# Flamingo block on one Trainium2 core: the first rounds' scores and weight splits and the last rounds' banks and VectorE list put in another order

## The chip, the cores and the metric

The kernel runs on one core of one Trainium2 chip. The metric is the device time of one execution in microseconds. The median of three timed runs counts; a profiled execution has its own time and a trace.

## The reference

For each of 32 batch entries (called tiles here: 128 tokens by 256 features) the reference computes two blocks, one behind the other:

```
x = x + tanh(g_xattn) * xattn(layernorm(x), ctx, ctx, mask)        # 16 heads of 16, called A
x = x + tanh(g_ffn)   * ffn(layernorm(x))                          # called B, below
ffn(y): q, k from rope(y), v from y; causal softmax attention, 16 heads; out projection
        x1 = layernorm(y + attention)
        gates = softmax(x1 @ gate_w.T + gate_b); the 2 largest of 8 are kept
        moe = sum over experts of gate_e * (x1 @ expert_w[e].T + expert_b[e])
        return layernorm(x1 + moe)
```

The softmax subtracts each row's maximum, and float32 accuracy is kept by splitting every operand of a large product into a high and a low part (three products in place of one).

## The kernel before

One tile is one batch entry. The work of a tile is cut into steps (a small function each), and each engine has one handwritten list of steps inside `for r in rounds`. A round advances two tiles; the 32 tiles take 21 rounds (r = 0 to 20), because a step of tile t stands in the round that its lag gives it (`scores("A", 2 * r - 1)`). A step for a tile below 0 or above 31 does nothing. So in the first and last rounds most of the list is empty, and `if r == ...` lines put things there that exist only at that end. Every engine works strictly in its list's order; semaphores say what a step waits for.

Names of the steps, with the tile in brackets behind them in this text: A0 is cross attention of tile 0, B31 causal attention of tile 31.

- Scores need the four **score banks** of PSUM (banks 0 to 3), one tile's attention at a time, in the fixed order A, B, A, B (`SCORES`). For each: ScalarE *seeds* the banks with the mask (`seed_scores`), TensorE adds the scores (`scores`, L516), VectorE takes the maxima (`maxima`, L1022), for A ScalarE seeds again with the transposed mask (`seed_scores_t`, L785), TensorE makes the transposed scores (`scores_t`, L535), the maxima are cast into two bfloat16 parts (`max_parts`, L1034 and L1036), transposed (`transpose_max`, L546, and `max_transposed`, L818), subtracted (`subtract_max`, L556), and ScalarE takes the exponentials (`exponentials`, L826). Only then can the next seed overwrite the banks.
- The four **work banks** (4 to 7) hold everything else: projections, products with the values (`attend`, L574, kept by `raw_values`, L834), `normalise` (L585), the expert products (`expert_pair`, L395). `WORK_USES` fixes their order; `take_work` waits until the last reader of the bank is done.
- **Splits**: each of the 16 weight matrices (Ak, Av, Aq, Ao, Bk, Bq, Bv, Bo, E0 to E7) arrives in one of six staging buffers; ScalarE makes the high part (`split_high`, L750), VectorE the low part (`split_low`, L933). They happen in the first rounds only. SyncE's queue loads a weight when the buffer's last low part is made.
- **keep_busy** (L411): products of the identity with itself, into a free work bank, whose result nobody reads. They stand where TensorE would be idle.
- After B's output projection (`project_o`, `finish_b`), the steps of a tile are: `statistics("1")`, GpSimd's `inverse_root`, `apply_u` (L964), GpSimd's `scale_shift_u`, `u_transposed` and its parts, `gate` (L595 on TensorE, L1077 on VectorE), `gate_rank`, `gate_choice`, `transpose_gates`, `gates_low` (L1115), `expert_bias_sum`, `bias_sum` (L1122), four `expert_pair` and eight `expert_sum` (L1131), `statistics("2")`, `apply_v` (L964, v_n) and `finish` on GpSimd, then the store. `rope` stands on GpSimd between `apply_y` (yn) and `rope_transposed`.

Of the kernel before, what the change touches and what calls it, by code (L numbers as in the profile page):

```python
# [30 lines left out]
PAIR = 2  # L31
# [104 lines left out]
def build(nc, dram, out):  # L136
    tiles = out.shape[0]
    with ExitStack() as ctx:
# [98 lines left out]

        def work_bank(use, n):

            key = (use, None) if (use, None) in WORK_AT else (use, n % PAIR)  # L240
            return work_banks[WORK_USES[WORK_AT[key]][2]]

        def work_last(use, n):
# [4 lines left out]
            while turn >= 0:  # L248
                _, half, other_bank, behind, readers = WORK_USES[turn % len(WORK_USES)]
                pair = turn // len(WORK_USES) - behind  # L250
                if other_bank == bank and live(PAIR * pair):
# [133 lines left out]
        def tensor_program(pe):  # L385
            def take_work(use, t):
                for name, value in work_last(use, t):
                    pe.wait_ge(sem[name], value)
                return work_bank(use, t)
# [40 lines left out]
            def u_transposed(t):  # L430
# [3 lines left out]
                transpose_two(take_work("u_t", t), u[t % U_SLOTS], "u_t", t)  # L434
# [192 lines left out]
            for r in rounds:  # L627
                gate(2 * r - 6)
                project_v_b(2 * r - 4)
                if r == 1:  # L630
                    keep_busy("x_t", 2, 3)
# [4 lines left out]
                project_o("B", 2 * r - 5)  # L636
                attend("B", 2 * r - 4)
                scores("A", 2 * r - 1)
                if r == 18:
                    keep_busy("gates_t", 30, 4)  # L640
                transpose_gates(2 * r - 6)
                expert_pair(0, 2 * r - 6)
                expert_bias_sum(2 * r - 6)
                expert_pair(1, 2 * r - 6)
                expert_pair(2, 2 * r - 6)
                if r == 1:
                    keep_busy("A_v", 2, 15)
                if r == 2:
                    keep_busy("A_v", 4, 13)
                scores_t("A", 2 * r - 1)  # L650
                transpose_max("A", 2 * r - 1)
                rope_transposed(2 * r - 2)
                subtract_max("A", 2 * r - 1)
                normalise("B", 2 * r - 4)
                expert_pair(3, 2 * r - 6)
                o_transposed("B", 2 * r - 4)
                if r == 1:
                    keep_busy("A_v", 2, 4)
                attend("A", 2 * r - 1)
                u_transposed(2 * r - 5)  # L660
                y_transposed(2 * r - 3)
                if r == 2:
                    keep_busy("A_v", 4, 4)
# [3 lines left out]
                project_k_a(r)  # L667
                if r == 18:
                    keep_busy("pair0", 31, 8)
                gate(2 * r - 5)  # L670
                normalise("A", 2 * r - 1)
                project_v_a(2 * r)
# [3 lines left out]
                transpose_max("B", 2 * r - 3)  # L676
                o_transposed("A", 2 * r - 1)
                if r == 0:
                    keep_busy("A_max_t", 0, 6)
                x_t(2 * r + 1)  # L680
# [7 lines left out]
                project_q_a(r)  # L688
# [5 lines left out]
                if r == 1:  # L694
                    keep_busy("rope_t", 1, 3)
# [6 lines left out]
                expert_bias_sum(2 * r - 5)  # L702
# [770 lines left out]
```

## Time and profile before

| what | value |
|---|---|
| median of 3 runs | 829.06 us (829.02 to 829.14) |
| the profiled execution's own time | 831.21 us |
| its span, first to last instruction | 829.5 us |
| PE (TensorE matmul) busy | 779.7 us, 94% of the span |
| DVE (VectorE) busy | 667.5 us, 80% |
| ACT (ScalarE) busy | 564.4 us, 68% |
| POOL (GpSimd) busy | 473.0 us, 57% |
| mean granted TensorE clock | 0.994 of full speed |

Times in the trace are microseconds from the start of the span. The busy share of PE includes the keep_busy products, so a busy PE is not yet a PE that sets the time. A row of the timeline gives start, duration, engine, line and operation; what stands in brackets is the idle time ahead of it on its engine and who ended it.

### The profile page before, as it was taken

How to read it: one execution, taken by the hardware profiler on the slowest of the kernel's cores; microseconds unless marked ns; L12 is line 12 of the kernel's file. 1: busy time of each engine (PE TensorE's matmuls, PEld its weight loads, DVE VectorE, ACT ScalarE, POOL GpSimd, SP SyncE). 2: the span in 40 equal slices, each digit the busy share in tenths (PEclk: the TensorE clock that was granted, in tenths of full speed). 3: DMA queues.
4: the chain of work that ended last, by engine and by line, in shares of the span. 5: the costliest groups of instructions: out<-in, count | busy, mean ns of one | idle time of the engine just before them, and what ended most of it. 6: DMA issues, size and time to landing. Idle time of an engine off the chain costs nothing.

```text
span 829.5 us, 24325 instructions
## 1 busy us (share of the span) xinstructions
PE 779.7 (94%) x9515; PEld 611.9 (74%) x9515; DVE 667.5 (80%) x1908; ACT 564.4 (68%) x1268; POOL 473.0 (57%) x854
## 2 busy tenths in 40 slices
PE   8888989999999999999999999999999999999896
PEld 4465768777787787778787788778778777777663
DVE  5756668797978979797988979797988979787876
ACT  5786767777786777777776777678677777764320
POOL 8434535566665646566574646566564655555343
PEclk9999999999999999999999999999999999999999
DMA  7510000010100101010100101010010000000000
GB/s 202 159 39 16 2 17 16 8 37 9 37 8 2 37 8 36 9 36 9 29 16 2 38 8 37 8 37 9 10 35 2 9 8 8 9 8 8 8 7 20
DMA packets 33570, 20.75 MB, mean 25 GB/s; under 512 B 11672, under 2 KB 33456, under 8 KB 33456
## 3 DMA queue, kind: packets, MB, share of 16 engines
q1 hardware_dynamic: 33456, 19.19, 8.1%
q8 instruction: 76, 1.25, 0.6%
q14 instruction: 38, 0.31, 0.1%
HBM read 14.99 MB, written 4.19 MB: 23 GB/s over the span
## 4 chain that ended last, share of the span: by engine, by line
PE 56%; ACT 24%; DVE 14%; issue 4%; POOL 1%; DMA 0%; SPq 0%; DVEq 0%; POOLq 0%
PE bank L395 26%; PE bank L516 8%; PE bank L535 7%; ACT bank L776 6%; DVE neg_max_A L1022 6%; ACT bank L785 5%; DVE moe L1131 4%; ACT probs_B L826 3%; PE bank L556 3%; PE bank L585 3%; ACT probs_A L826 3%; PE bank L574 2%; PE bank L404 2%; ACT k_heads_B L809 2%; PE bank L546 1%
## 5 line engine op out<-in xcount | busy, mean ns | idle before, releaser
L1343 POOL TENSOR_SCALAR_AFFINE_SELECT probs_B<-probs_B 128x512 f32<-128x512 f32 x128 | 77.3, 640 | 184.4 <-ACT probs_B L826 184.4
L1131 DVE SCALAR_TENSOR_TENSOR moe<-bank,gates,moe 128x256 f32<-128x256 f32 x256 | 123.2, 481 | 48.2 <-PE bank L395 33.2
L785 ACT ACTIVATE bank<-mask_add 128x512 f32<-128x512 bf16 x128 | 76.6, 602 | 49.2 <-DVE neg_max_A L1022 49.2
L395 PE MATMUL bank<-w_expertsa,u_t_a 128*128 128x512 f32 x256 | 105.6, 413 | 0.1
L395 PE MATMUL bank<-w_expertsa,u_t_b 128*128 128x512 f32 x256 | 100.9, 394 | 0.0
L395 PE MATMUL bank<-w_expertsb,u_t_a 128*128 128x512 f32 x256 | 100.9, 394 | 0.0
L1022 DVE TENSOR_REDUCE neg_max_A<-bank 128x4 f32<-128x512 f32 x128 | 79.5, 684 | 11.9 <-PE bank L516 11.5
L1022 DVE TENSOR_REDUCE neg_max_B<-bank 128x4 f32<-128x512 f32 x128 | 79.3, 682 | 5.5 <-PE bank L516 5.5
L776 ACT ACTIVATE bank<-mask_add 128x512 f32<-128x512 bf16 x128 | 69.8, 626 | 0.0
L776 ACT ACTIVATE bank<-causal_add 128x512 f32<-128x512 bf16 x128 | 69.7, 623 | 0.0
L826 ACT ACTIVATE probs_A<-bank 128x512 f32<-128x512 f32 x128 | 66.1, 603 | 4.4 <-PE bank L556 2.2
L826 ACT ACTIVATE probs_B<-bank 128x512 f32<-128x512 f32 x128 | 66.2, 607 | 3.2 <-PE bank L556 1.1
L834 ACT ACTIVATE o_raw<-bank 128x512 f32<-128x512 f32 x64 | 38.5, 602 | 27.8 <-PE bank L574 27.8
L395 PEld LDWEIGHTS bank<-w_expertsa,u_t_a 128*128 128x128 f32 x256 | 49.1, 192 | 10.6 <-issue 0.4
L1260 POOL TENSOR_SCALAR var_eps<-mean_var 128x1 f32<-128x1 f32 x64 | 12.3, 192 | 77.7 <-DVE mean_var L960 75.2
L395 PEld LDWEIGHTS bank<-w_expertsa,u_t_b 128*128 128x128 f32 x256 | 48.1, 188 | 11.4
L395 PEld LDWEIGHTS bank<-w_expertsb,u_t_a 128*128 128x128 f32 x256 | 48.3, 189 | 6.7
L535 PEld LDWEIGHTS bank<-q_heads_A,k_heads_A 32*128 32x128 f32 x1024 | 31.4, 186 | 22.4 <-ACT bank L785 22.4
L809 ACT ACTIVATE k_heads_A<-bank,k_cols_A,head_rows 128x256 f32<-128x256 f32 x64 | 30.9, 565 | 23.0 <-PE bank L395 23.0
L535 PE MATMUL bank<-q_heads_A,k_heads_A 32*128 32x128 f32 x1024 | 37.5, 283 | 8.1 <-ACT bank L785 7.4
L411 PE MATMUL bank<-ident_bf 128*128 128x512 bf16 x167 | 42.7, 396 | 1.9 <-ACT k_heads_B L809 1.9
L516 PE MATMUL bank<-k_heads_A,q_heads_A 32*128 32x256 f32 x512 | 36.7, 399 | 5.8 <-ACT bank L776 4.7
(224 smaller groups left out, 2440.5 us busy)
## 6 DMA issues: line engine op xcount, KB each, us to landing
x_in<-in_x SPq DMA_DIRECT2D x32, 128.0 KB, 2.2
ctx_t<-in_ctxT SPq DMA_DIRECT2D x32, 128.0 KB, 2.2
out<-y_out SPq DMA_DIRECT2D x32, 128.0 KB, 1.7
w_stage<-in_expertsT SPq DMA_DIRECT2D x8, 256.0 KB, 4.3
mask_u<-in_masks SPq DMA_DIRECT2D x32, 32.0 KB, 2.1
w_stage<-in_in_projT SPq DMA_DIRECT2D x3, 256.0 KB, 4.8
w_stage<-in_WkT SPq DMA_DIRECT2D x1, 256.0 KB, 3.5
w_stage<-in_WvT SPq DMA_DIRECT2D x1, 256.0 KB, 3.6
```

The costliest lines, as they stand in the source:

```text
L395: done = pe.matmul(out_ap, l, r, start=n == 0, stop=n == len(terms) - 1)
L411: pe.matmul(bank[:], ident_bf[:], ident_bf[:].unsqueeze(1).to_broadcast([P, GROUP, P]), start=True, stop=True)
L516: done = pe.matmul(score_banks[g][:, c * 2 * P:(c + 1) * 2 * P], queries[strip, half, c, :], keys[strip, half, c, :, :], start=False, stop ...
L535: pe.matmul(score_banks[g][:, i * P:(i + 1) * P], keys[strip, half, c, odd, :], queries[strip, half, c, :], start=tag == "B" and i == 0, s ...
L776: act.activation(score_banks[g][:].rearrange("p (h k) -> p h k", k=P), mask[:, 0:1, :].to_broadcast([P, GROUP, P]), ACT.Copy).then_inc(sem ...
L785: act.activation(score_banks[g][:].rearrange("p (h k) -> p h k", k=P), mask_add[t % MASK_SLOTS][:, 1:2, :].to_broadcast([P, GROUP, P]), AC ...
L809: act.activation(k_heads[tag][pair % PAIR_SLOTS][:, :, c, odd, :], bank[:, c * PAIR * P:(c + 1) * PAIR * P].rearrange("p (j n) -> p j n", ...
L826: act.activation(probs[tag][:, g * GROUP:(g + 1) * GROUP, :].rearrange("p h q -> p (h q)"), score_banks[g][:], ACT.Exp, scale=SCALE).then_ ...
L834: act.activation(o_raw[:], work_bank(tag + "_values", t)[:], ACT.Copy).then_inc(sem[tag + "_or"], 1)
L1022: dve.tensor_reduce(neg_max[tag][:, g * GROUP:(g + 1) * GROUP], score_banks[g][:].rearrange("p (h k) -> p h k", k=P), AXIS_X, ALU.max, neg ...
L1131: dve.scalar_tensor_tensor(out=moe[(e + 1) % 2][:], in0=bank[:, (e % 2) * EMBED:(e % 2 + 1) * EMBED], scalar=gates[:, e:e + 1], in1=moe[e ...
L1343: pool.affine_select(out=part, in_=part, compare_op=ALU.is_ge, fill=0.0, base=0, pattern=[[0, GROUP], [1, P]], channel_multiplier=-1).then ...
```

## The change

It rewrites the lists at both ends; the rounds between stay as they are but for one wait on `u_transposed` that goes.

First rounds (r = 0 to 4). On TensorE the scores of A1 stand ahead of A0's output projection, transpose_max of A0 and A1 ahead of their scores_t, project_k_a(1) ahead of attend of A1, x_t(3) ahead of normalise of A1, rope_transposed(0) far behind, project_q_a(1) ahead of project_o of A1. keep_busy counts change (8 in place of 3 between that project_o and the scores of A2; 4 moved from ahead of B1's scores to ahead of A3's). On ScalarE and VectorE the splits and the gate's small parts move to other places.

Last rounds (r = 17 to 20). Six uses of work banks by the last tiles (`LATE`) go to score banks, which nobody seeds again. With that, tile 31's normalise, transpose, output projection and u_transposed move ahead on TensorE, and VectorE's list takes the steps of tiles 29 to 31 in a new order; GpSimd's `scale_shift_u` stands ahead of `finish` in r = 19.

```diff
+        LATE = {("B_normalise", tiles - 1): (0, "B_exp", GROUPS * tiles), ("B_o_t", tiles - 1): (1, "B_exp", GROUPS * tiles),
+                ("B_out", tiles - 1): (2, "B_exp", GROUPS * tiles), ("pair3", tiles - 3): (3, "B_exp", GROUPS * tiles),
+                ("u_t", tiles - 1): (0, "B_on", tiles), ("gate", tiles - 1): (1, "B_ot_b", tiles)}
+
         def work_bank(use, n):
 
+            if (use, n) in LATE:
+                return score_banks[LATE[use, n][0]]
...
             def take_work(use, t):
+                if (use, t) in LATE:
+                    pe.wait_ge(sem[LATE[use, t][1]], LATE[use, t][2])
+                    return work_bank(use, t)
...
                 pe.wait_ge(sem["u"], t + 1)
-                transpose_two(take_work("u_t", t), u[t % U_SLOTS], "u_t", t)
+                transpose_two(work_bank("u_t", t), u[t % U_SLOTS], "u_t", t)
...
                 if r == 1:
-                    keep_busy("x_t", 2, 3)
+                    keep_busy("x_t", 2, 2)
+                if r == 1:
+                    scores("A", 2 * r - 1)
                 project_o("A", 2 * r - 2)
...
                 attend("B", 2 * r - 4)
-                scores("A", 2 * r - 1)
...
+                if r == 2:
+                    keep_busy("A_v", 4, 4)
+                if r != 1:
+                    scores("A", 2 * r - 1)
...
                 y_transposed(2 * r - 3)
-                if r == 2:
-                    keep_busy("A_v", 4, 4)
                 scores("B", 2 * r - 3)
...
                 if r == 1:
-                    keep_busy("rope_t", 1, 5)
+                    keep_busy("A_values", 2, 3)
+                if r == 1:
+                    project_q_a(r)
                 project_o("A", 2 * r - 1)
...
                 if r == 1:
-                    keep_busy("rope_t", 1, 3)
+                    keep_busy("A_values", 2, 8)
...
                 if r == 18:
                     keep_busy("pair1", 31, 3)
                 expert_bias_sum(2 * r - 5)
+                if r == 17:
+                    normalise("B", 2 * r - 3)
                 expert_pair(1, 2 * r - 5)
...
+                if r == 17:
+                    o_transposed("B", 2 * r - 3)
...
                 expert_pair(3, 2 * r - 5)
+                if r == 17:
+                    u_transposed(2 * r - 4)
+                if r == 17:
+                    project_o("B", 2 * r - 3)
...
+                if use == "u_t" and t >= tiles - 2:
+                    act.wait_ge(sem[read[0]], read[1] * t)
...
+                if t == tiles - 2:
+                    dve.wait_ge(sem["vn"], t)
                 dve.tensor_tensor(moe[0][:], work_bank("bias", t)[:, 0:EMBED], u[t % U_SLOTS][:], ALU.add).then_inc(
                     sem["moe"], 1)
```

**ScalarE (ACT), tiles 0 and 1.** The rows from the transposed maxima of A0 to the exponentials of A1 (neg_max_t, probs, o_raw; L776 is the seed, L785 the second seed, L750 a high split; xn_t_a belongs to tile 2, rope_t_a to tile 0). Before:

```order
L750 ACTIVATE w_Aoa<-w_stage 128x512
L750 ACTIVATE w_Bka<-w_stage 128x512
L750 ACTIVATE w_Bqa<-w_stage 128x512
L750 ACTIVATE w_Bva<-w_stage 128x512
L818 ACTIVATE neg_max_t_A<-bank 128x128
L826 ACTIVATE probs_A<-bank 128x512 x4
L834 ACTIVATE o_raw<-bank 128x512
L750 ACTIVATE w_Boa<-w_stage 128x512
L756 ACTIVATE o_t_A_a<-bank 128x256
L776 ACTIVATE bank<-mask_add 128x512 x4
```

Of the change:

```order
L807 ACTIVATE w_Bqa<-w_stage 128x512
L894 ACTIVATE o_raw<-bank 128x512
L836 ACTIVATE bank<-mask_add 128x512 x4
L816 ACTIVATE o_t_A_a<-bank 128x256
L807 ACTIVATE w_Bva<-w_stage 128x512
L807 ACTIVATE w_Boa<-w_stage 128x512
L822 ACTIVATE xn_t_a<-bank 128x2x128
```

The seed of A1 (L836 there) moved ahead of A0's output, and two splits went from before the seed to behind it.

**VectorE (DVE), from the statistics of round 2 to the maxima of B0.** neg_max_A is A2's, yn is tile 1's, w_expertsb is a low split, rope_t_b is tile 1's, y_t_b tile 0's. Before:

```order
L964 TENSOR_SCALAR yn<-x_1,mean_var_B,rstd_B 128x256
L1022 TENSOR_REDUCE neg_max_A<-bank 128x4 x4
L1034 CAST neg_max_bf_A<-neg_max_A 128x4x16
L1036 TENSOR_TENSOR neg_max_bf_A<-neg_max_A,neg_max_bf_A 128x4x16
L933 TENSOR_TENSOR w_expertsb<-w_stage,w_expertsa 128x2x256 x2
L979 TENSOR_TENSOR rope_t_b<-bank,rope_t_a 128x2x128
L971 TENSOR_TENSOR y_t_b<-bank,y_t_a 128x256
L1022 TENSOR_REDUCE neg_max_B<-bank 128x4 x4
```

Of the change:

```order
L1091 TENSOR_REDUCE neg_max_A<-bank 128x4 x4
L1033 TENSOR_SCALAR yn<-x_1,mean_var_B,rstd_B 128x256
L1002 TENSOR_TENSOR w_expertsb<-w_stage,w_expertsa 128x2x256
L1103 CAST neg_max_bf_A<-neg_max_A 128x4x16
L1105 TENSOR_TENSOR neg_max_bf_A<-neg_max_A,neg_max_bf_A 128x4x16
L1002 TENSOR_TENSOR w_expertsb<-w_stage,w_expertsa 128x2x256 x2
L1048 TENSOR_TENSOR rope_t_b<-bank,rope_t_a 128x2x128
L1002 TENSOR_TENSOR w_expertsb<-w_stage,w_expertsa 128x2x256 x5
L1040 TENSOR_TENSOR y_t_b<-bank,y_t_a 128x256
L1091 TENSOR_REDUCE neg_max_B<-bank 128x4 x4
```

yn(1) moved behind the maxima of A2, one low split between them and the cast, and five low splits (E3 to E7) ahead of B0's maxima. On ScalarE the high parts of E4 and E5 stand ahead of A2's exponentials, and those of E6 and E7 behind y_t_a(0), which follows q_heads of B0.

**VectorE, the end of tile 30's gate to its expert sums.** u_n is tile 31's, stats<-moe and v_n are tile 29's in the change, gates_t, bias and sums (moe) tile 30's. Before:

```order
L1107 TENSOR_SCALAR gates<-chosen,gate_inv 128x3x8
L1069 TENSOR_TENSOR u_n<-bank,base_B 128x256
L952 BN_STATS stats<-u_n 128x6
L1115 TENSOR_TENSOR gates_t<-bank,gates_t 32x128
L960 BN_AGGR mean_var<-stats 128x2
L1122 TENSOR_TENSOR moe<-bank,u 128x256
L1131 SCALAR_TENSOR_TENSOR moe<-bank,gates,moe 128x256 x3
L964 TENSOR_SCALAR u_n<-u_n,mean_var,rstd 128x256
L1131 SCALAR_TENSOR_TENSOR moe<-bank,gates,moe 128x256 x5
L952 BN_STATS stats<-moe 128x6
```

Of the change:

```order
L1176 TENSOR_SCALAR gates<-chosen,gate_inv 128x3x8
L1021 BN_STATS stats<-moe 128x6
L1029 BN_AGGR mean_var<-stats 128x2
L1033 TENSOR_SCALAR u_n<-u_n,mean_var,rstd 128x256
L1184 TENSOR_TENSOR gates_t<-bank,gates_t 32x128
L1033 TENSOR_SCALAR v_n<-moe,mean_var,rstd 128x256
L1193 TENSOR_TENSOR moe<-bank,u 128x256
L1202 SCALAR_TENSOR_TENSOR moe<-bank,gates,moe 128x256 x6
L1040 TENSOR_TENSOR u_t_b<-bank,u_t_a 128x256
L1202 SCALAR_TENSOR_TENSOR moe<-bank,gates,moe 128x256 x2
```

finish_b and the statistics of tile 31 moved into tile 30's gate, ahead of these rows; the application of tile 31's norm moved ahead of the gates' low part. The same pattern stands once more at the end: behind tile 31's gates come statistics("2", 30), apply_v(30) and only then the gates' low part of tile 31.

## Rows read from the trace of the kernel before

**Rows 1.** The page's first line.
```profile
span 829.5 us, 24325 instructions
```
**Rows 2.** Timeline of ACT: the same seed in two neighbouring middle rounds (start, duration).
```profile
635.23 2.18 ACT L776 ACTIVATE bank<-mask_add 128x512 f32<-128x512 bf16 x4
...
682.40 2.18 ACT L776 ACTIVATE bank<-mask_add 128x512 f32<-128x512 bf16 x4
```
**Rows 3.** Chain that ended last, first rounds (start, duration, what).
```profile
21.54 0.52 ACT w_Bqa L750
...
23.23 2.06 ACT probs_A L826 x4
...
38.45 2.06 ACT probs_A L826 x4
...
49.76 1.18 PE bank L516 x16
...
56.24 2.06 ACT probs_A L826 x4
...
64.16 2.48 DVE neg_max_B L1022 x4
```
**Rows 4.** Timeline of ACT, the values of A0 and the seed of A1.
```profile
26.05 0.60 ACT L834 ACTIVATE o_raw<-bank 128x512 f32<-128x512 f32 x1 [0.76 <-PE bank L574]
...
28.97 2.15 ACT L776 ACTIVATE bank<-mask_add 128x512 f32<-128x512 bf16 x4
```
**Rows 5.** Timeline of DVE around the maxima of A2 and B0.
```profile
53.44 0.70 DVE L1034 CAST neg_max_bf_A<-neg_max_A 128x64 bf16<-128x64 f32 x1
...
54.80 1.48 DVE L933 TENSOR_TENSOR w_expertsb<-w_stage,w_expertsa 128x512 fp32r<-128x512 f32 x2
...
63.23 0.42 DVE L971 TENSOR_TENSOR y_t_b<-bank,y_t_a 128x256 fp32r<-128x256 f32 x1 [6.62 <-ACT y_t_a L756]
...
67.03 0.13 DVE L1034 CAST neg_max_bf_B<-neg_max_B 128x64 bf16<-128x64 f32 x1
```
**Rows 6.** Timeline of POOL, first and last operation of rope(1).
```profile
50.40 0.73 POOL L1293 TENSOR_TENSOR roped<-yn,rope_cos 128x256 f32<-128x256 f32 x1
...
52.21 0.72 POOL L1299 TENSOR_TENSOR roped<-roped,rope_tmp 128x256 f32<-128x256 f32 x1
```
**Rows 7.** Timeline of PE: keep_busy x8, scores of A3, scores_t of B29.
```profile
59.63 1.90 PE L411 MATMUL bank<-ident_bf 128*128 128x512 bf16 x8
...
73.06 1.15 PE L516 MATMUL bank<-k_heads_A,q_heads_A 32*128 32x256 f32 x16 [0.47 <-ACT bank L776]
...
747.85 1.93 PE L535 MATMUL bank<-q_heads_B,k_heads_B 32*128 32x128 f32 x32 [1.27 <-DVE neg_max_B L1022]
```
**Rows 8.** Stretches around it: busy time by engine, then the granted clock (PEclk), DMA share, GB/s.
```profile
747.00:747.50 0.50, 0.00 (x0) 0.00 (x0) 0.50 (x2) 0.00 (x0) 0.00 (x0) 1.00 0.00 0
748.50:749.00 0.50, 0.50 (x16) 0.50 (x16) 0.49 (x3) 0.30 (x2) 0.00 (x0) 0.50 0.00 0
```
**Rows 9.** Timeline of DVE, last rounds: tile 31 from its norm to its result.
```profile
809.64 0.41 DVE L964 TENSOR_SCALAR u_n<-u_n,mean_var,rstd 128x256 f32<-128x256 f32 x1
...
812.83 0.43 DVE L952 BATCH_NORM_STATS2 stats<-moe 128x6 f32<-128x256 f32 x1
...
814.49 0.17 DVE L1077 TENSOR_TENSOR logits<-bank,gate_bias 128x8 f32<-128x8 f32 x1 [0.70 <-PE bank L595]
...
816.32 0.23 DVE L1107 TENSOR_SCALAR gates<-chosen,gate_inv 128x24 f32<-128x24 f32 x1
...
817.29 0.28 DVE L1115 TENSOR_TENSOR gates_t<-bank,gates_t 32x128 fp32r<-32x128 f32 x1 [0.41 <-ACT gates_t L840]
...
822.25 1.07 DVE L1131 SCALAR_TENSOR_TENSOR moe<-bank,gates,moe 128x256 f32<-128x256 f32 x2 [0.25 <-PE bank L395]
823.36 0.43 DVE L952 BATCH_NORM_STATS2 stats<-moe 128x6 f32<-128x256 f32 x1
...
825.02 0.73 DVE L964 TENSOR_SCALAR v_n<-moe,mean_var,rstd 128x256 f32<-128x256 f32 x1 [1.02 <-POOL rstd L1263]
```

More of the change, by code:

```diff
@@ L248, in work_last @@
             while turn >= 0:
-                _, half, other_bank, behind, readers = WORK_USES[turn % len(WORK_USES)]
+                other, half, other_bank, behind, readers = WORK_USES[turn % len(WORK_USES)]
                 pair = turn // len(WORK_USES) - behind
-                if other_bank == bank and live(PAIR * pair):
+                if other_bank == bank and live(PAIR * pair) and (half is None or (other, PAIR * pair + half) not in LATE):
                     m = pair if half is None else PAIR * pair + half
@@ L657, in tensor_program @@
                 if r == 1:
-                    keep_busy("A_v", 2, 4)
+                    keep_busy("A_v", 2, 3)
+                if r == 1:
+                    project_k_a(r)
                 attend("A", 2 * r - 1)
-                u_transposed(2 * r - 5)
+                if r != 18:
+                    u_transposed(2 * r - 5)
                 y_transposed(2 * r - 3)
-                if r == 2:
-                    keep_busy("A_v", 4, 4)
                 scores("B", 2 * r - 3)
@@ L676, in tensor_program @@
                 transpose_max("B", 2 * r - 3)
+                if r == 1:
+                    keep_busy("rope_t", 0, 3)
+                if r == 1:
+                    rope_transposed(2 * r - 2)
                 o_transposed("A", 2 * r - 1)
@@ L716, in tensor_program @@
                 expert_pair(3, 2 * r - 5)
+                if r == 17:
+                    u_transposed(2 * r - 4)
+                if r == 17:
+                    project_o("B", 2 * r - 3)
                 project_q_b(r - 1)
-                if r == 17:
-                    keep_busy("u_t", 30, 5)
-                normalise("B", 2 * r - 3)
-                u_transposed(2 * r - 4)
+                if r != 17:
+                    normalise("B", 2 * r - 3)
+                if r != 17:
+                    u_transposed(2 * r - 4)
                 if r == 1:
@@ L1185, in vector_program @@
                 add_values("B", 2 * r - 5)
+                if r == 2:
+                    maxima("A", 2 * r - 2)
                 apply_y(2 * r - 3)
@@ L1189, in vector_program @@
                 gates_low(2 * r - 7)
-                maxima("A", 2 * r - 2)
+                if r == 2:
+                    split_low("E0")
+                if r != 2:
+                    maxima("A", 2 * r - 2)
+                if r == 18:
+                    apply_u(2 * r - 6)
                 bias_sum(2 * r - 7)
@@ L1194, in vector_program @@
                 expert_sum(1, 2 * r - 7)
+                if r == 18:
+                    inverse_sums("B", 2 * r - 5)
+                if r == 18:
+                    normalise("B", 2 * r - 5)
                 expert_sum(2, 2 * r - 7)
```

262 lines of the change are left out of this document (182 added, 80 removed).

## The prediction

> **What bounds the kernel now.** I read the page's first line, then the seeds of two neighbouring middle rounds. The span is 829.5 us [rows 1], and the same seed starts at 635.23 and again at 682.40 [rows 2], so two tiles cost 47.17 us, and the change leaves the middle lists alone except for a wait on u_transposed. The transposition right behind it (y_transposed) waits for a later count of the same kind of reader, so I cost that at nothing. A gain can therefore only be an offset: the moment at which the steady pattern starts (I take the scores of A3) moves, or the stretch behind the last seed gets shorter. Next I followed the chain of waits through the first rounds [rows 3]. It alternates between ACT, PE and DVE: exponentials of A0 at 23.23, of A1 at 38.45, scores of A2 at 49.76, exponentials of A2 at 56.24, maxima of B0 at 64.16. Then come the scores of A3 at 73.06 [rows 7]. Gains made early count only as far as they survive to that row. Last I read DVE's timeline of the end [rows 9].
>
> The profiled execution took 831.21 us with a span of 829.5; the three timed runs have a median of 829.06. I make the sum as a difference and apply it to the median.
>
> **First rounds, step by step.**
>
> A0 and A1. Of the four high splits ahead of A0's exponentials two remain; each takes 0.52 [rows 3]. Two are 1.04, so the exponentials move from 23.23 to 22.2. The values of A0, read at 26.05 to 26.65 [rows 4], are read at 25.05 to 25.65. The seed of A1 started only at 28.97 [rows 4], behind a split and A0's output parts; now it follows at once, at 25.6: 3.4 earlier. PE's fillers let the scores follow by the same 3.4. The two splits that went behind that seed do not stand ahead of A1's exponentials in the old place, which gives a little more: I take 4.2 (between 3.4 and 3.4 + 1.04 = 4.4) and put the exponentials of A1 at 34.25 instead of 38.45.
>
> Scores of A2. From 38.45 to 49.76 were 11.31 us. PE has five more keep_busy there (8 for 3). Eight take 1.90 [rows 7], so five take 1.19. PE waits a little for the query heads there, so I take 0.85 of it: 34.25 + 11.31 + 0.85 = 46.4. The gain has shrunk to 3.3 (3.0 with the full 1.19).
>
> Exponentials of A2. The cast of its maxima started at 53.44, 3.68 behind the scores. Two paths lead on. On DVE: maxima done at 46.4 + 3.68 = 50.1, then yn(1) (0.41 as the like operation in [rows 9]), one low split (two took 1.48 [rows 5], so 0.74), and from the cast to the exponentials 56.24 - 53.44 = 2.80 as before: 54.05. The cast took 0.70 beside GpSimd's work and 0.13 alone [rows 5], which could give 0.57 back. On GpSimd: yn(1) stood ahead of the maxima and now stands behind them, so rope(1) starts only at about 50.5. It takes 52.21 + 0.72 - 50.40 = 2.53 [rows 6] and ends at 53.0; rope_transposed stands ahead of A2's subtraction on PE, and its high part (ACT) as well as the high splits of E4 and E5 stand ahead of the exponentials. With 0.3 for the transposition, 0.38 or so for the part and one split of 0.52 not hidden: 54.2. The second path ends last: 54.2 instead of 56.24, a gain of 2.0. So the new wait for rope(1) takes 1.3 of the 3.3.
>
> Maxima of B0. y_t_b(0) stood at 63.23 and the maxima behind it at 64.16, DVE having idled 6.62 us for y_t_a [rows 5]. With the gain of 2.0, y_t_a is done at 61.2. Behind it on ACT stand the high splits of E6 and E7 (2 x 0.52), to 62.25; the low split of E7 ends 0.69 to 0.74 later, at 62.95; y_t_b takes 0.42 and the maxima start at 63.35. Five low splits cost 5 x 0.74 = 3.7 us of DVE; three of them lie in those 6.62 us of idle time and are free, the last is not, because it waits for ACT. The gain shrinks to 0.85. If splits 6 and 7 were hidden (scores of B0 late), it would stay 2.0.
>
> Scores of A3. PE idled 0.47 us ahead of them for the seed [rows 7]; four keep_busy (0.95) stand there now. 0.95 - 0.47 = 0.48 would be lost if the attend before them stays where it is, nothing if PE has more room. I take 0.35: **0.85 - 0.35 = 0.5 us gained**, and bounds from 1.6 gained (splits half hidden, keep_busy free) to 0.1 lost.
>
> **Last rounds, step by step.** The last tile's normalise, transposition and projection go to score banks and no longer wait for the work banks, so PE is some 3 us earlier with them. What follows is DVE's list. The norm of tile 31 was applied at 809.64 [rows 9]; it waits for GpSimd's inverse root, behind that of tile 29, and I put it at about 807.0. Then u of tile 31 goes through GpSimd and two transpositions, and DVE meets tile 30's eight sums, whose last ones wait for the last expert pair of tile 30 on PE. They ended at 812.83. Now u_t_b (0.42) stands ahead of the last two, so the logits start at 813.25, not 814.49: 1.2 gained. From the logits to the end of the gates is 816.32 + 0.23 - 814.49 = 2.06 [rows 9]: 815.3. There the gain is given back. statistics of tile 30, GpSimd's root and v_n(30) stand now ahead of gates_low(31). In the same form at the end this takes 825.02 - 823.36 = 1.66 to the start of v_n [rows 9], and v_n takes 0.41: 815.3 + 1.66 + 0.41 = 817.4, or 817.15 with the handovers overlapped as DVE overlaps its rows. Before, gates_low started at 817.29. The bias product, the last three pairs on PE and the last two sums (822.25, waiting for PE [rows 9]) hang on it. I take **0 for the tail**, bounds 0.25 gained (the 0.25 of PE idle at the last sums) to 0.3 lost.
>
> Sum: 829.06 - 0.5 - 0 = 828.5 (rounded). A measurement of this kernel can tell about 0.2%, 1.66 us, from no change, so this is "the same". Own range 827.2 to 829.5.
>
> **The clock.** B29's transposed scores are a warning: PE had idled 1.27 us for the maxima [rows 7], the granted clock was 1.00 before (2.4 GHz) and 0.50 behind it (1.2 GHz) [rows 8], and the 32 products took 1.93 us, where the 16 scores products of the same bytes take 1.15 [rows 7]. The change makes holes of this size: one of about 1.3 us ahead of B0's subtraction, and one of about 1.9 us near 806 where the bias product of tile 30 waits for gates_low behind tile 31's norm. The Trainium skill ("TensorE: Matmul & The Clock Gate", section "HAM oscillation — how this bites in real kernels") gives as abstract rule that only PE gaps of several microseconds throttle. By that rule these holes would cost nothing and the sum would stay 828.5; this trace does not agree, its gap was 1.27 us.
>
> **Rivals.**
> A, the front gain survives: if rope(1) or the E6/E7 splits are not on the path (GpSimd starts earlier; maxima of B0 are late anyway), the 3.3 us at A2's scores reach A3 in full or nearly: 829.06 - 3.3 = 825.8, and with half of it lost 827.4. For it: DVE's 6.62 us of idle time [rows 5]. Against: the order of the list puts ACT's two splits between y_t_a and the maxima.
> B, slower: a hole behind which the clock falls. At B0 it costs 1.93 - 1.15 = 0.8 on the products and 0.1 on the subtraction: 828.5 + 0.9 = 829.4. In the tail, with expert products of tiles 30 and 31 at half speed for some microseconds, 1.0 to 1.9: 829.5 to 830.4. Both: 830.4 to 831.3. It decides from where PE idles about 1.3 us with little work ahead of it. For it: [rows 7, 8]. Against: the keep_busy products that stand near both places.
> C, it does not do what it says: the score banks free PE, but the end is set by tile 31's gate and DVE's list, which is a tail of 0. That is part of the likeliest case already; if DVE's holes in tile 30's gate close better than I read, the tail gives 1.2 more: 827.3.
>
> **How the numbers follow.** Likeliest case (828.5; 827.2 to 829.5) 0.43; A 0.27 (825.4 to 827.4); B 0.20 (half of it at 830.4 and above); others, C's better tail among them, 0.10. The range 825.4 to 830.8 leaves out about 0.2. Faster than 827.4: all of A, 0.27, and 0.09 from the others and the likeliest's edge: 0.36. Slower than 830.7: half of B and a little, 0.13. The rest, 0.51, is the same.
>
> **What would show it.** Exponentials of A0 at 22.2, of A1 near 34.3, scores of A2 near 46.4; rope(1) starting behind A2's maxima and PE's subtraction waiting for it; exponentials of A2 near 54.2; DVE's maxima of B0 at 63.35 with a low split ended just before y_t_b; scores of A3 at 72.6; a round of 47.17; u_n(31) 2.7 earlier than 809.64, logits(31) 1.2 earlier, gates_low(31) unmoved, each less the front's offset. Granted clock of 0.50 near 60 to 69 or 806 to 812 would be rival B. The prediction is wrong if the offset at A3 is over 1.6, or if the round's length changes.

## The result, and the profile after

The changed kernel takes 832.18 us in the median (831.90 to 833.87, five runs) against 829.14 for the kernel before, measured beside it. The ratio is 1.0036, 95% interval 1.0023 to 1.0048: slower by 3.0 us. I had forecast 828.5, with a wider range of 825.4 to 830.8. The profiled execution took 832.16 us with a span of 830.4.

First the chain of waits of the changed kernel through the first rounds; it answers to [rows 3], [rows 5] and [rows 6].

```profile
46.96 1.11 PE bank L526 x16
...
50.53 0.33 DVE yn L1033
...
50.94 1.11 POOL roped L1433
...
53.12 1.01 POOL roped L1439
...
55.55 4.63 PE bank L405 x24
...
62.56 0.53 ACT w_expertsa L807
...
63.11 1.29 DVE w_expertsb L1002 x2
64.40 0.34 DVE y_t_b L1040
64.73 2.40 DVE neg_max_B L1091 x4
...
73.10 0.97 PE bank L421 x4
74.07 1.11 PE bank L526 x16
```

The reader is to see that the order of the waits is the one foretold: yn(1), rope(1) on GpSimd, the splits, y_t_b(0), the maxima. Two sizes are not. rope(1) takes 3.2 us (50.94 to 54.13) and not 2.53. VectorE's splits and cast run beside it here; in the run yn_first below the same rope(1) runs beside VectorE's maxima and takes 2.54 again. And the 24 products behind it take 4.63 us. In the kernel before the same 24 stood from 56.67 to 59.63 [rows 7], 2.96 us; its row of TensorE's timeline is

```profile
56.67 0.39 PE L395 MATMUL bank<-rope_t_a,w_Bka 128*128 128x256 f32 x1 [0.46 <-DVE rope_t_b L979]
```

Why they take longer, these stretches of the changed kernel show (busy time by engine, then the granted clock):

```profile
53.50:54.00 0.50, 0.00 (x0) 0.00 (x0) 0.50 (x2) 0.50 (x2) 0.50 (x1) 1.00 0.08 25
56.00:56.50 0.50, 0.50 (x4) 0.50 (x4) 0.50 (x2) 0.50 (x3) 0.50 (x1) 0.50 0.87 241
57.00:57.50 0.50, 0.50 (x5) 0.50 (x4) 0.50 (x2) 0.50 (x3) 0.50 (x1) 0.50 0.84 262
60.00:60.50 0.50, 0.50 (x5) 0.25 (x4) 0.00 (x0) 0.50 (x3) 0.00 (x0) 1.00 0.63 124
```

TensorE ran at 1.2 GHz (0.50) there, at 2.4 GHz (1.00) ahead and behind. Such a stretch at 0.50 is called a fall of the clock below. Its timeline shows what it did before: it idled, for rope(1) and then for the low part of its transposition.

```profile
54.17 0.33 PE L414 MATMUL bank<-ident,roped 128*128 128x128 f32 x1 [1.29 <-POOL roped L1439]
...
55.55 0.42 PE L405 MATMUL bank<-rope_t_a,w_Bka 128*128 128x256 f32 x1 [0.60 <-DVE rope_t_b L1048]
```

So the scores of A3 stand at 74.07 and not at 73.06 [rows 7]. The offset stays: the seeds of the middle rounds are 0.96 us late at 92.62 (91.66 before) and 1.02 at 683.42 [rows 2], so the round is as long as it was.

Next VectorE's timeline of the end, which answers to [rows 9].

```profile
806.98 0.41 DVE L1033 TENSOR_SCALAR u_n<-u_n,mean_var,rstd 128x256 f32<-128x256 f32 x1 [1.86 <-POOL rstd L1403]
807.43 0.28 DVE L1184 TENSOR_TENSOR gates_t<-bank,gates_t 32x128 fp32r<-32x128 f32 x1
...
813.64 0.16 DVE L1146 TENSOR_TENSOR logits<-bank,gate_bias 128x8 f32<-128x8 f32 x1
...
815.46 0.23 DVE L1176 TENSOR_SCALAR gates<-chosen,gate_inv 128x24 f32<-128x24 f32 x1
...
817.26 0.73 DVE L1033 TENSOR_SCALAR v_n<-moe,mean_var,rstd 128x256 f32<-128x256 f32 x1 [1.02 <-POOL rstd L1403]
818.02 0.28 DVE L1184 TENSOR_TENSOR gates_t<-bank,gates_t 32x128 fp32r<-32x128 f32 x1
...
824.32 0.43 DVE L1021 BATCH_NORM_STATS2 stats<-moe 128x6 f32<-128x256 f32 x1
```

The last statistics stand at 824.32, those of the kernel before at 823.36: 0.96 later, the same number as the offset of the front. Read this way the tail costs nothing, as I had said. But that is a coincidence, and the profiled executions differ by 0.95 us (832.16 and 831.21) where the medians differ by 3.0. The other 2.1 us are in the profile of before itself. Its execution took 831.21 us where the median is 829.06, and its trace has two falls of the clock while TensorE still works, [rows 8] and this one:

```profile
803.00:803.50 0.50, 0.50 (x4) 0.50 (x3) 0.43 (x3) 0.25 (x2) 0.00 (x0) 0.50 0.00 0
```

The first cost 1.09 us. ScalarE's timeline has the seeds of B29, B30 and B31, of the kernel before:

```profile
741.81 2.18 ACT L776 ACTIVATE bank<-causal_add 128x512 f32<-128x512 bf16 x4
...
758.96 2.15 ACT L776 ACTIVATE bank<-causal_add 128x512 f32<-128x512 bf16 x4
...
776.02 2.15 ACT L776 ACTIVATE bank<-causal_add 128x512 f32<-128x512 bf16 x4
```

and of the changed kernel, whose clock stayed up there:

```profile
742.87 2.18 ACT L836 ACTIVATE bank<-causal_add 128x512 f32<-128x512 bf16 x4
758.93 2.15 ACT L836 ACTIVATE bank<-causal_add 128x512 f32<-128x512 bf16 x4
...
776.00 2.15 ACT L836 ACTIVATE bank<-causal_add 128x512 f32<-128x512 bf16 x4
```

From the seed of B29 to that of B30 it is 758.96 - 741.81 = 17.15 us in the one and 758.93 - 742.87 = 16.06 in the other. So this fall used up the offset of the front: the last seeds stand at the same time, and the 0.96 us at the last statistics are all of the last rounds. What the second fall cost, an end of the old list without one must show; the first experiment has it.

### The profile page after: what moved, and what is told of

Read it like the earlier page. It is cut to its first block, busy times and chain, and to the rows that moved or that the text cites. A ratio compares the mean times of both kernels' runs of the same rounds, so it can differ in the third digit from the quotient of the medians.

```text
span 830.4 us, 24286 instructions
## 1 busy us (share of the span) xinstructions
PE 776.4 (93%) x9510; PEld 611.4 (74%) x9510; DVE 666.2 (80%) x1908; ACT 564.3 (68%) x1268; POOL 472.4 (57%) x854
## 4 chain that ended last, share of the span: by engine, by line
PE 54%; ACT 23%; DVE 15%; issue 4%; POOL 2%; SPq 1%; DMA 0%; DVEq 0%; POOLq 0%
PE bank L405 24%; PE bank L526 8%; PE bank L545 7%; ACT bank L836 6%; DVE neg_max_A L1091 6%; ACT bank L845 5%; DVE moe L1202 4%; ACT probs_B L886 3%; PE bank L595 3%; PE bank L566 3%; ACT probs_A L886 3%; PE bank L584 2%; ACT k_heads_B L869 2%; PE bank L414 2%; PE bank L556 1%
## 5 line engine op out<-in xcount | busy, mean ns | idle before, releaser
L836 ACT ACTIVATE bank<-mask_add 128x512 f32<-128x512 bf16 x128 | 69.8, 625 | 0.0
L836 ACT ACTIVATE bank<-causal_add 128x512 f32<-128x512 bf16 x128 | 69.7, 623 | 0.0
L869 ACT ACTIVATE k_heads_A<-bank,k_cols_A,head_rows 128x256 f32<-128x256 f32 x64 | 30.9, 564 | 22.2 <-PE bank L405 22.2
L1433 POOL TENSOR_TENSOR roped<-yn,rope_cos 128x256 f32<-128x256 f32 x32 | 24.2, 756 | 30.1 <-DVE yn L1033 30.1
```

What stands on the lines that cost most here:

```text
L836: act.activation(score_banks[g][:].rearrange("p (h k) -> p h k", k=P), mask[:, 0:1, :].to_broadcast([P, GROUP, P]), ACT.Copy).then_inc(sem ...
L869: act.activation(k_heads[tag][pair % PAIR_SLOTS][:, :, c, odd, :], bank[:, c * PAIR * P:(c + 1) * PAIR * P].rearrange("p (j n) -> p j n", ...
```

## The experiments

All differ from the kernels shown by the edits named. Beside the medians the lowest times are given, because an execution is about 1.1 us longer for each fall of the clock in it (last section), and the lowest time has the fewest. The kernel before was measured anew beside the experiments, on the same chip, and the ratios are against those times.

**The two halves.** front_only is the change's r = 0 to 4 with the old last rounds; tail_only the reverse, and it has the wait that goes from the middle rounds too.

> The change's first rounds (r = 0 to 4) with the last rounds of the kernel before. Theory 1 (the front loses about 1.0 us, the tail about 2.0): the seeds of the middle rounds stand 1.0 us later than in the kernel before, as in the changed kernel (92.62 against 91.66), the clock falls to 0.50 near 56 to 59, and the time is 829.1 + 1.0 = 830.1 us. Rival 1 (all of the 3 us comes from the front or from the middle rounds and the tail is neutral): 832.1. Rival 2 (the front alone is neutral and the offset comes from somewhere the tail's edits reach, such as the banks): 829.1.

Measured: 831.14 us against 830.24, ratio 1.0009 (0.9999 to 1.0019), lowest 829.83 against 829.27. The lowest times differ by 0.6 us and the medians by 0.9; the interval just includes no change, so the times alone do not prove the front's loss. In the trace the middle seeds are late by 2.1 us (93.74 against 91.66), more than in the changed kernel with the same list, since the clock stayed low for longer, from 54.5 to 61.5. No fall of the clock is behind that until TensorE is done, so its end is undisturbed. The last seed in ScalarE's timeline, then rows of VectorE's:

```profile
776.74 2.15 ACT L812 ACTIVATE bank<-causal_add 128x512 f32<-128x512 bf16 x4
```

```profile
814.12 0.17 DVE L1119 TENSOR_TENSOR logits<-bank,gate_bias 128x8 f32<-128x8 f32 x1 [0.70 <-PE bank L603]
...
815.96 0.23 DVE L1149 TENSOR_SCALAR gates<-chosen,gate_inv 128x24 f32<-128x24 f32 x1
816.11 0.40 DVE L1006 TENSOR_SCALAR v_n<-moe,mean_var,rstd 128x256 f32<-128x256 f32 x1
816.92 0.28 DVE L1157 TENSOR_TENSOR gates_t<-bank,gates_t 32x128 fp32r<-32x128 f32 x1 [0.41 <-ACT gates_t L876]
...
822.97 0.43 DVE L994 BATCH_NORM_STATS2 stats<-moe 128x6 f32<-128x256 f32 x1
```

So the last statistics are 46.23 us behind the last seed. In the changed kernel they are 824.32 - 776.00 = 48.32 behind it, in the profile of before 823.36 - 776.02 = 47.34. The low clock at 803 had cost 1.1 us, and the change's own last rounds cost **2.1**. The gates' low part of tile 31 stood 816.92 - 815.96 = 0.96 us behind the gates; in the changed kernel it stands 2.56 behind them. The logits of tile 31 stood 37.38 us behind the last seed and stand 37.64 behind it.

> The kernel before with only the change's last rounds (six bank uses in the score banks, the new lists of r = 17 to 20). Theory 1: the seeds up to 741.81 stand exactly as before, and the rest is about 2.0 us longer than in an execution of the kernel before whose clock stays at full speed: 831.1 us. Rival (tail neutral, as I predicted): 829.1. Rival (tail gains its 1.2 us at the logits): 827.9.

Measured: 832.89 against 830.24, ratio 1.0030 (1.0018 to 1.0042). Its span is 831.0 with one fall of the clock at 748; from the last seed (776.59) to the end 54.4 us, as in the changed kernel, against 829.1 - 776.74 = 52.4 with the old list. The traces of the runs further down agree: 54.4 in splits_late and fill, which have the new last rounds unrepaired and no fall of the clock there, 52.3 and 52.4 in front_fix and front_best, which have the old ones. The neutral tail is refuted. My 831.1 was too low, by that fall of the clock and by 0.6 us that the seeds were already late (742.38 against 741.81) though the list up to there is the old one; why they were is not known.

**The front: late rope or low clock.** In yn_first only this moved in the changed kernel:

```diff
+                apply_y(2 * r - 3)
                 if r == 2:
                     maxima("A", 2 * r - 2)
-                apply_y(2 * r - 3)
```

> The changed kernel with yn(1) back ahead of the maxima of A2 on VectorE, nothing else. VectorE idles 1.31 us ahead of these maxima, so yn(1) (0.40) fits and the maxima stay at 48.05. Theory 1 (rope(1), late behind yn(1), makes the hole of 1.29 and 0.60 us on PE behind which the clock fell from 55.9 to 59.1, about 1.4 us, besides 0.7 of plain waiting): rope(1) starts near 47.9, no row with clock 0.50 near 56, the middle seeds 1.4 to 2.1 us earlier than in the changed kernel, time 832.2 - 1.7 = 830.5 (830.1 to 830.8). Rival (the chain through B0 is set by the splits E6 and E7 and by keep_busy, the clock is nothing): under 0.5 us, 831.7 or more.

Measured in the trace: no low clock in the front. The hole did not go, though. TensorE no longer waits for rope(1), which runs from 48.32 to 50.86, but for the two parts behind it, and idles 1.37 us (TensorE's timeline):

```profile
54.82 0.39 PE L405 MATMUL bank<-rope_t_a,w_Bka 128*128 128x256 f32 x1 [1.37 <-DVE rope_t_b L1048]
```

From the chain of waits:

```profile
61.16 0.53 ACT w_expertsa L807
...
61.71 1.29 DVE w_expertsb L1002 x2
63.01 0.34 DVE y_t_b L1040
63.34 2.40 DVE neg_max_B L1091 x4
...
72.68 1.11 PE bank L526 x16
```

The maxima of B0 stand at 63.3 and the scores of A3 at 72.7: the values that the prediction had given for the change itself (63.35 and 72.6). The seeds gain 1.4 us at once (91.23 against 92.62). The time did not follow: 833.35, ratio 1.0037 (1.0023 to 1.0050). In the profiled execution (833.32) the clock fell twice in the tail, near 807 to 811 and 818 to 822, and from the last seed to the end it took 56.7 us and not 54.4; for the other executions this cause is taken over from that one. The expected 830.5 is a miss. The trace of the front confirms that rope(1)'s place is worth 1.4 us; it does not confirm that a hole of this size always brings the clock down.

splits_late has the low splits of E6 and E7 directly behind the maxima of B0.

```diff
                     split_low("E5")
+                low_part("y_t", y_t, "y_t", 2 * r - 4)
+                maxima("B", 2 * r - 4)
+                if r == 2:
                     split_low("E6")
                     split_low("E7")
-                low_part("y_t", y_t, "y_t", 2 * r - 4)
-                maxima("B", 2 * r - 4)
```

> The changed kernel with VectorE's low splits of E6 and E7 moved from ahead of y_t_b(0) to behind the maxima of B0, nothing else. Theory 1 (two splits of together 1.29 us stand between y_t_a at 62.55 and y_t_b at 64.32): y_t_b near 62.6, the maxima of B0 are then held by the scores only and start near 63.15 instead of 64.65; the middle seeds come up to 1.5 us earlier, less what the low parts now put in front of the attend and the normalisation behind: time 832.2 - 1.2 = 831.0 (830.7 to 831.6). Rival (the chain to A3 is set by TensorE's own list and keep_busy): 832.2, unchanged.

Measured: 833.45, ratio 1.0036 (1.0024 to 1.0049): nothing gained. VectorE's timeline:

```profile
63.37 2.48 DVE L1091 TENSOR_REDUCE neg_max_B<-bank 128x4 f32<-128x512 f32 x4 [0.21 <-PE bank L526]
65.77 1.28 DVE L1002 TENSOR_TENSOR w_expertsb<-w_stage,w_expertsa 128x512 fp32r<-128x512 f32 x2
...
67.47 0.13 DVE L1103 CAST neg_max_bf_B<-neg_max_B 128x64 bf16<-128x64 f32 x1
```

The maxima came 1.28 us earlier, and the same two splits then stood ahead of their cast, which starts at 67.47 and not at 67.54. A stall that is moved from ahead of an operation to behind it, ahead of its consumer, is not gone. The theory's 1.2 us were wrong. The rival had the time nearly right (832.07 is the lowest), but not the reason: it was not keep_busy that held the chain, but the cast.

fill leaves every wait as it is and gives TensorE work in the two holes:

```diff
+                if r == 1:
+                    keep_busy("A_values", 2, 5)
                 rope_transposed(2 * r - 1)
                 subtract_max("A", 2 * r)
+                if r == 1:
+                    keep_busy("A_values", 2, 2)
```

> The changed kernel with seven more keep_busy products in round 1, five ahead of rope_transposed(1), where TensorE idled 1.29 us for GpSimd, and two behind A2's subtraction, where it idled 0.60 us for rope_t_b. They take nothing out of the chain: rope(1) is as late as before. Theory 1 (the clock falls because of these holes and its fall alone cost the 24 products 4.62 - 2.96 = 1.7 us): the granted clock stays 1.00 from 54 to 60, the 24 products take about 3.0 us, y_t_a comes 0.9 to 1.7 us earlier (keep_busy and k_heads stand ahead of it), the scores of A3 stand at 72.9 to 73.2 instead of 74.07, and the time is 0.9 to 1.2 us under the changed kernel's lowest. Rival (the late rope is the cost, and the low clock was hidden behind ScalarE's k_heads_B): the clock is restored and the scores of A3 move by under 0.3 us.

Measured, the same two stretches as above:

```profile
56.00:56.50 0.50, 0.50 (x7) 0.50 (x6) 0.50 (x2) 0.50 (x3) 0.50 (x1) 1.00 0.84 232
57.00:57.50 0.50, 0.50 (x6) 0.50 (x6) 0.50 (x2) 0.50 (x3) 0.50 (x1) 1.00 0.93 259
```

And the chain of waits of fill:

```profile
64.08 2.40 DVE neg_max_B L1095 x4
...
73.41 1.11 PE bank L526 x16
```

With rope(1) as late as in the changed kernel (its last operation at 53.09) the clock stayed at 1.00, and the maxima of B0 came 0.65 us and the scores of A3 0.66 us earlier. So of the 1.4 us between the changed kernel and yn_first, the low clock is 0.65: TensorE waits 0.58 us for ScalarE's k_heads_B in fill, which hides the rest of its 1.67 us. The late rope(1) is the other 0.7. That lies between what theory 1 (72.9 to 73.2) and the rival (under 0.3 us) had for the scores of A3. The time was 833.69, ratio 1.0049 (1.0034 to 1.0063): no gain. The profiled execution, at 832.49 the fastest, had the clock low near 748 to 752. How far the filling kept the clock up in the front is open, since there is one trace of fill: with the two holes unfilled the clock fell in all three traces (the changed kernel, front_only, splits_late), but holes of this size go both ways elsewhere (last section).

**The tail, edit by edit,** each on tail_only. t_gates31 puts gates_low(31) ahead of v_n(30) (r == 19), t_u31 puts gates_low(30) ahead of apply_u(31):

```diff
-                if t == tiles - 2:
+                if t >= tiles - 2:
                     dve.wait_ge(sem["vn"], t)
...
-                apply_v(2 * r - 8)
+                if r != 19:
+                    apply_v(2 * r - 8)
...
                 gates_low(2 * r - 7)
+                if r == 19:
+                    apply_v(2 * r - 8)
...
+                gates_low(2 * r - 6)
                 if r == 18:
                     apply_u(2 * r - 5)
-                gates_low(2 * r - 6)
```

The first three pieces are t_gates31 (with the first, bias_sum(31) waits for v_n(30)), the last is t_u31; t_both has all.

> The kernel before with the change's last rounds, but gates_low(31) ahead of v_n(30) on VectorE (and bias_sum(31) waits for v_n(30), as it must). In tail_only the gates of tile 31 were made 62.86 us and gates_low(31) started 65.4 us... counted from the last seed: gates at 39.45, gates_low at 42.02, against 39.22 and 40.18 in the last rounds of the kernel before. Theory 1 (v_n(30), which waits 1.0 us for GpSimd's root, holds the gates' low part 1.6 us): gates_low near 40.6, bias_sum near 42.0 instead of 42.78, the sums end 0.8 to 1.2 us earlier, the time is about 1.0 us under that of tail_only. Rival (the end is set by the expert pairs on TensorE, which would move too little, or by VectorE's eight sums behind v_n): 0.3 us or less.

(62.86 and 65.4 in that text are slips; the rows are the 39.45 and 42.02 that follow them.)

> The kernel before with the change's last rounds, but apply_u(31) behind gates_low(30) on VectorE. Theory 1 (norm 31's application waits 1.86 us for GpSimd's root and holds gates_low(30), behind which TensorE idles 2.06 us for the bias product of tile 30): gates_low(30) moves from 31.42 to about 29.9 behind the last seed, the hole on TensorE shrinks to about 0.6 us, bias_sum(30) comes 0.3 us earlier at most, because v_n(29) stands behind both: the time is 0.2 to 0.4 us under tail_only's. Rival (this order is the whole loss of 2 us): 2 us under tail_only.

> Both edits of the two runs above together, on the kernel before with the change's last rounds. Theory 1: the losses add, 1.2 to 1.4 us under tail_only, which leaves the last rounds 0.6 to 0.8 us longer than those of the kernel before. Rival (score banks and the earlier projection gain once VectorE's list no longer waits): as fast as the kernel before or faster, 829.1 where that takes 829.1.

Measured: t_gates31 830.68 (ratio 1.0005, 0.9996 to 1.0013), t_u31 831.21 (1.0013, 1.0005 to 1.0022), t_both 830.22 (1.0000, 0.9990 to 1.0010). The lowest times are 829.64, 830.07 and 829.05, against 828.64 for the kernel before on that chip. The two together remove most of the loss and leave 0.4 us; from the last seed to the end t_both takes 827.4 - 774.62 = 52.8 us, 1.6 less than tail_only (the theory had 1.2 to 1.4). In the traces the edit of t_u31 brings the logits of tile 31 from 37.64 to 36.98 behind the last seed, 0.66 us and not the 0.2 to 0.4 of its theory, since TensorE's hole ahead of tile 30's bias product goes from 2.06 to 0.69 us. That is 0.4 us earlier than the old list has them (37.38), so up to there the rest of the new last rounds gains that much. The edit of t_gates31 gives 1.05 us from the gates to the last statistics, as its theory had it. In t_both the bias sum of tile 31 still stands 2.66 us behind the gates, against 1.72 with the old list (817.68 - 815.96 in front_only), because v_n(30), which it has to wait for, itself waits 0.55 us for GpSimd's root:

```profile
815.22 0.75 DVE L998 TENSOR_SCALAR v_n<-moe,mean_var,rstd 128x256 f32<-128x256 f32 x1 [0.55 <-POOL rstd L1353]
816.08 0.42 DVE L1158 TENSOR_TENSOR moe<-bank,u 128x256 f32<-128x256 f32 x1
```

The norm of tile 31 waits for GpSimd too:

```profile
804.66 0.28 DVE L1149 TENSOR_TENSOR gates_t<-bank,gates_t 32x128 fp32r<-32x128 f32 x1 [0.93 <-ACT gates_t L871]
805.58 0.41 DVE L998 TENSOR_SCALAR u_n<-u_n,mean_var,rstd 128x256 f32<-128x256 f32 x1 [0.64 <-POOL rstd L1353]
```

t_swap puts, in r = 19, inverse root 1(31) ahead of inverse root 2(29) on GpSimd.

```diff
+                if r == 19:
+                    inverse_root("1", 2 * r - 7, "un")
                 inverse_root("2", 2 * r - 9, "vn")
...
-                inverse_root("1", 2 * r - 7, "un")
+                if r != 19:
+                    inverse_root("1", 2 * r - 7, "un")
```

> t_both with GpSimd's inverse root 1(31) ahead of inverse root 2(29). In t_both root 1(31) was made at 30.93 behind the last seed because root 2(29) stood ahead and its input came only at 29.10; mean_var 1(31) was there at 28.18. Theory (the list on GpSimd, not the score banks, holds tile 31's norm): u_n(31) at about 29.1 instead of 30.96, v_n(29) near 30.4, bias_sum(30) at 30.8 instead of 31.80, and all behind it 1.0 us earlier: 1.0 us under t_both's lowest, so 0.6 us under the kernel before's. Rival (TensorE's pairs of tile 30, which wait for the sums to free the banks, or u_t(31), set it): 0.3 us or less.

Measured: 828.95 against 830.08, ratio 0.9992 (0.9983 to 1.0000); lowest 828.71 against 828.79; last seed to end 827.1 - 774.90 = 52.2 us. It gained 0.6 us over t_both in the trace, not 1.0: gates_low(30) waits for ScalarE (0.94 us) and the rest queues behind it. The lowest time is 0.1 us under the kernel before's, where 0.6 was expected. With these repairs the score banks' tail is as fast as the old one and hardly faster (52.4 there).

**Repairs put together.** front_fix is front_only with yn(1) first and the two splits behind o_t_A_b(2). front_best has them behind max_parts of A3, and the four keep_busy back behind y_transposed(1). best is the changed kernel with front_best's front and t_swap's tail.

> The change's first rounds with yn(1) back ahead of the maxima of A2 and the low splits of E6 and E7 moved behind o_t_A_b(2) on VectorE, past everything that the exponentials of B0 and the attend of B0 wait for; last rounds of the kernel before. Theory 1: with yn(1) first the scores of A3 stood at 72.68 (73.06 before); the splits give back up to 1.29 us more, of which the keep_busy products and the seed of A3 let 0.8 to 1.2 through: seeds of the middle rounds 1.2 to 1.6 us earlier than in the kernel before, time 1.2 to 1.6 us under it. Rival (TensorE's list with four keep_busy sets A3 whatever the maxima do): 0.4 us under it. Rival (the splits' new place holds values_B(0) or the maxima of A3): no gain or a loss.

> front_fix with two more edits: the low splits of E6 and E7 stand behind max_parts of A3 (in front_fix GpSimd's causal masks of B0 took 2.97 us beside them and 2.42 without), and the four keep_busy products go back from ahead of A3's scores to behind y_transposed(1). Theory: 0.55 + 0.97 us less, of which the seed of A3 at 70.98 lets all through: scores of A3 near 71.1 instead of 72.18, the middle seeds 1.0 us earlier than front_fix's, the lowest time 1.8 us under the kernel before's. Rival (the shorter filling of TensorE brings the clock down, or the splits hold the parts of A3): no gain over front_fix.

> The changed kernel with all repairs: yn(1) first, the two low splits behind max_parts of A3, the four keep_busy back, gates_low(31) ahead of v_n(30), apply_u(31) behind gates_low(30), GpSimd's root 1(31) ahead of root 2(29). Theory: the gains of front_best and t_swap add: 1.8 + 0.6 = 2.4 us under the kernel before's lowest time and 5 us under the changed kernel's. Rival: the sum is less because another hole of TensorE near the end brings a clock fall of about 1.1 us.

Measured: front_fix 828.89 against 829.86 (ratio 0.9989, 0.9979 to 0.9999), front_best 827.96 against 830.08 (0.9977, 0.9966 to 0.9988), best **826.97 against 830.08 (0.9966, 0.9953 to 0.9979)**. The lowest time of front_fix is 1.4 us under the kernel before's (827.20 against 828.64), within its theory. Those of front_best and best are 826.73 and 826.78 against 828.79: 2.1 and 2.0 us, where 1.8 and 2.4 were expected. So the gains of the two ends did not add; the front gives nearly all. In its profiled execution best has the scores of A3 at 72.39 and not at 71.4 as front_best. Everything from the first scores on was late (17.48 against 16.03); the changed kernel, whose list is the same up to there, has them at 16.05, so that is not of the edit. In front_best and best, TensorE still waits 1.36 us for rope_t_b and the clock falls behind it, in front_fix it waits as long and the clock stays up. The row of best:

```profile
55.78 0.39 PE L405 MATMUL bank<-rope_t_a,w_Bka 128*128 128x256 f32 x1 [1.36 <-DVE rope_t_b L1048]
```

The 24 products take 4.64 us there, so there may be more to be had; that hole was not filled in any run.

## Why the prediction was wrong, point by point

- **The front up to the scores of A2** was right: exponentials of A0 at 22.23 (22.2), of A1 at 34.19 (34.25), scores of A2 at 46.89 (46.4). From the exponentials of A1 to there it took 12.70 us, 1.39 more than before; I had 0.85, and the five keep_busy alone are 1.19.
- **Exponentials of A2**: 54.98 against 54.2. The mechanism was right, rope(1) was mis-sized: 3.2 us, not 2.53. That is 0.65 of the 0.8; it also started 0.4 late with the scores of A2, and the way from its end to the exponentials was 0.3 shorter than I had it.
- **Maxima of B0**: 64.65 against 63.35, and with it the step "scores of A3: 0.5 us gained", which became 1.0 lost. 0.8 of the 1.3 at the maxima is the late rope(1) carried on, and the step left out that the new wait of TensorE for it is itself a hole behind which the clock can fall; fill has the fall at 0.65 us. I had put a hole ahead of B0's subtraction into rival B and priced it at 0.9; the fall was behind A2's instead. yn_first meets my numbers (63.34 and 72.68), but not by my mechanism: in it rope(1) is early and the clock stayed up.
- **Length of the round**: right; so was the wait on u_transposed at nothing.
- **Last rounds, "I take 0 for the tail"**: this failed most. The step that failed is "1.2 gained" at the logits. The norm of tile 31 came as foretold (806.98; 807.0), but the rows it was set against were of an execution that the low clock at 803 had made 1.1 us later there. Against an end without a fall the logits are 0.26 us later, not 1.2 earlier. I had read 831.21 beside 829.06 and taken it for an offset that cancels; it does not, because the events that made the difference lie in the very rows of the comparison. What was to be given back was mis-sized too: v_n(30) took 0.73 us and not 0.41, as the last row of [rows 9] shows for the same form, so gates_low(31) stands at 818.02 and not at 817.15 to 817.4, and 1.6 us are lost from the gates to it, not 1.1 to 1.3. With 0.26 at the logits and 0.25 in the last sums the term is 2.1 us lost. The repairs split it otherwise than where it shows: v_n(30) behind gates_low(31) gives back 1.05, apply_u(31) behind gates_low(30) 0.66, and 0.4 stays.
- **The clock as a rival** (B) had a mechanism that exists, but it explains only 0.65 of the 3.5 us between forecast and result; the falls that it expected in the tail did not come in the changed kernel's trace (its two runs at 833.65 and 833.87 may have had one). In the traces here the clock fell behind holes of 1.27 us, of 1.29 and 0.60, of 1.36 and of 2.04, though not each time. The Trainium skill's rule ("TensorE: Matmul & The Clock Gate", section "HAM oscillation — how this bites in real kernels"), by which only gaps of several microseconds throttle, does not agree with that.

The sum with the measured terms, made afterwards: 829.1 + 1.0 + 2.1 = 832.2; measured 832.18. The 1.0 is of the one profiled execution and has a fall of the clock in it; in front_only, with the same list, it was 2.1.

## What to carry to other kernels

If the profiled execution is slower than the median, find where in its trace the difference lies before using rows near it as a baseline. When a producer is put behind something (yn behind the maxima), price the whole chain that hangs on it on the other engines, and look at what TensorE does meanwhile: a short wait can cost as much behind it as in it (0.65 and 0.7 us here). On an in-order engine an operation that waits for a slow round trip (here v_n behind GpSimd's root) belongs behind the one that another engine waits for, and moving work from ahead of an operation to directly behind it gains nothing if the consumer's next step stands there too.

## What the runs showed of the hardware

The times of one kernel can lie in steps. On the chip of t_both the 34 runs of the kernel before were 828.64 to 829.12 us (12 runs, clock 0.997 to 0.999), 829.75 to 830.12 (12 runs, 0.995 to 0.998) and 830.85 to 832.23 (10 runs, 0.994 to 0.995). The changed kernel's five runs were 831.90 to 832.18 (0.996) and 833.65 to 833.87 (0.992 to 0.994). On the two other chips of the experiments the steps are blurred. A step of about 1.1 us is what one fall of the clock near 748 (1.09 us) or near 803 (1.1 us) costs; that each step is one fall is argued from this size, since one execution of each kernel has a trace.

What decides that the clock falls in one execution and not in the next stays open. The length of the hole alone does not. All 14 traces have a hole of 1.27 us ahead of B29's transposed scores; the clock fell behind it in four (the kernel before, tail_only, splits_late, fill). Of the four traces with a hole of 1.36 or 1.37 us ahead of the 24 products it fell in two (front_best and best, not yn_first and front_fix), of the six with 2.04 to 2.07 us ahead of the bias product of tile 30 in two (yn_first and t_gates31). The fall near 803 in the kernel before had only holes of 0.59 and 0.41 us close ahead of it. In the changed kernel TensorE idled 2.05 us there and the clock stayed at 1.00. The stretch from 808 of the changed kernel:

```profile
808.00:810.00 2.00, 2.00 (x11) 1.65 (x11) 1.69 (x4) 0.00 (x0) 1.92 (x4) 1.00 0.00 0
```

The same stretch of yn_first:

```profile
808.00:810.00 2.00, 2.00 (x8) 1.52 (x7) 1.69 (x4) 0.00 (x0) 1.92 (x3) 0.50 0.00 0
```

That is also why a repair of 1.4 us in the front did not show in the profiled execution of yn_first.

GpSimd's rope of 128x256 float32 values took 2.53 us in the kernel before and 2.54 in yn_first, beside VectorE's maxima of the score banks, and 3.2 in the changed kernel, beside VectorE's subtractions of 128x512.
